# A hybrid attention kernel: where in a tick TensorE adds the logits of the additive attention

## The chip, the cores and the metric

One Trainium2 chip, one of its cores. The metric is the device time of one execution in microseconds (us). Of the kernel before there are three timed runs and one profiled execution. The profiler names the engines PE (TensorE, matrix products), PEld (its weight loads), DVE (VectorE), ACT (ScalarE), POOL (GpSimd) and SP (SyncE, which here only issues DMAs).

## The reference

The input is 16 batches of 768 tokens with 128 channels. Three layers follow one another, each with a residual:

```python
x = x + _L0_conv_ref(_gn(x), ...)        # group norm, 8-head attention with two relative biases and a causal mask
t = t + _L1_attn_ref(_ln_t(t), ...)      # additive attention, below
t = t + _L1_ffn_ref(_ln_t(t), ...)       # 8 experts, top 2, gathered and scattered rows
```

The part that the change touches is the additive attention. With hidden width 16 it computes, for every pair of tokens of a batch:

```python
A = jnp.einsum('bse,he->bsh', q, W1[:, :e]) + b1
B = jnp.einsum('bse,he->bsh', k, W1[:, e:])
hidden = jnp.tanh(A[:, :, None, :] + B[:, None, :, :])
logits = jnp.einsum('bijh,h->bij', hidden, w2) + b2[0]
attn = jax.nn.softmax(logits, axis=-1)
return jnp.einsum('bij,bjd->bid', attn, v)
```

## The kernel before

**Passes, ticks, quarters.** The batches run through a software pipeline of five stages, `pre`, `max`, `mid`, `add` and `end`. A pass handles one stage of each of five consecutive batches; passes 1 to 12 hold all five stages, those before and after hold fewer. A pass is cut into 24 ticks, a tick into four quarters (slot 0 to 3). Every engine walks the ticks in its own program order and meets the others only at semaphores, so "the same tick" may lie several microseconds apart on two engines. After the passes comes the expert part, which the change leaves alone.

**What PE does in a tick.** In each quarter it makes the ring uses that `tick_order` deals out (`fill`): matrix products and transposes into three PSUM banks used in turn. They are called here by their names in the code: `max` (products whose maximum bounds the first attention's scores, L1113), `heads` and `headsT`, `project`, `probsT` (transposes of the second attention's probabilities, L1132), `attended` (their product with the values, L1135), and so on. Behind the uses of quarters 0 and 1 stands half a step of the first attention's scores (`fill_scores`, L1005 and L1008). In quarter 2 stands `weigh_values` (L1021), the product of probabilities and values of the first attention.

**The query groups.** The logits of the additive attention are made for 24 groups q of 32 queries in a pass. POOL adds (`sums`, L833) three quarters of the hidden layer of group q at its tick q, ACT takes the tanh (L954, and L960, which does the last quarter whole) at its tick q, and PE multiplies by w2 (`add_logits`, L1035) at its tick q + 1. `add_logits` has 8 matmuls of 384 columns, each an output strip of 32 columns of the array; `weigh_values` has 4 matmuls in strips of the same kind. All other products use the array's full width. Four groups fill one PSUM region: q % 4 == 0 starts it and waits for ACT's exponential of the four before (`exp_logits`, L938), q % 4 == 3 ends it, after which DVE takes its maximum at slot 1 of the next tick. In the kernel before, groups with q % 4 of 1, 2 and 3 are added at the start of slot 0, those with q % 4 == 0 in slot 2, ahead of `weigh_values`. So with t = q + 1, ticks 1, 5, 9, 13, 17 and 21 have the addition in slot 2, the other eighteen in slot 0.

**The waits around it.** A ring use waits until DVE has read the bank used three uses earlier; `headsT` waits for DVE's reading of `heads`, `attended` for that of `probsT`. Half a score step waits until ACT has taken the exponential (`exp_scores`, L931) of the same half of the step before: ACT does that at the start of its tick, before its tanh. POOL's `sums` of group q wait for the logits of group q - 4, since `hidden` has four slots. At tick 1 SP stores the last block of the `end` batch and then, at tick 2, issues the loads of `q_max`, `k_max`, `q_parts` and `k_parts` (L650); at ticks 0 to 5 and 18 to 23 POOL also issues indirect DMAs of rows (L862), with a drain ahead of the third sum.

Of the kernel before, what the change touches and what calls it, by code (L numbers as in the profile page):

```python
# [47 lines left out]
def score_step(t, first):  # L48

    for stage in ("max", "mid"):  # L50
        d = TICKS * STAGES.index(stage) + t - first
        if 0 <= d < len(STEPS):
            return stage, d
    return None, None
# [58 lines left out]
def tick_order(t):  # L113

    units = list(MAX_AT[t])
    uses = list(AT[t])
    step = max(1, len(units) // max(1, len(uses)))
    out = []
    while units or uses:
        out += units[:step]  # L120
        units = units[step:]
        for _ in range(1 if len(uses) <= 3 else 2):
            if uses:
                out.append(uses.pop(0))
    n = len(out)
    return [out[n * i // PARTS:n * (i + 1) // PARTS] for i in range(PARTS)]
# [37 lines left out]
def positive(count):  # L164

    return not isinstance(count, int) or count > 0


def hybrid_kernel(nc, x, Wq0, Wk0, Wv0, Wo0, rel_t, rel_n, Wq1, Wk1, Wv1, W1, b1, w2, b2,
# [38 lines left out]
    with ctx:  # L208
# [764 lines left out]
        def _(pe):  # L973
# [38 lines left out]
            def weigh_values(c, side, d):  # L1012
                quad, lo, kb, q0, n_ = STEPS[d]
                pe.wait_ge(scores_read, c * 48 + (2 * d + 2))
                group = sum(g < d for g in LAST_OF_GROUP)
                if kb == 0:

                    if positive(count := c * 6 + group):
                        pe.wait_ge(av_copied, count)
                for g in range(4):  # L1020
                    last = mm(av_bank[32 * g:32 * g + 32, q0 - lo:q0 - lo + n_], v_aug[:, side, kb, 4 * quad + g, :],  # L1021
                              probs0[:, d % 3, g, 0:n_], start=(kb == 0), stop=(d in LAST_OF_GROUP),
                              skip_group_check=True)
                last.then_inc(av_done, 1)

            def add_logits(b, q):
                k = q % 4
                pe.wait_ge(tanh_done, b * 24 + (q + 1))
                if k == 0:

                    if positive(count := b * 6 + q // 4):
                        pe.wait_ge(probs1_ready, count)
                for half in range(2):
                    for g in range(4):
                        last = mm(logits[32 * g:32 * g + 32, half, 0:HALF], w2_shifted[:, k, :],  # L1035
                                  hidden[:, q % SLOTS, g, HALF * half:HALF * half + HALF], start=(k == 0), stop=(k == 3))
                last.then_inc(logits_added, 1)

            def keep_warm(n):
                for _ in range(n):  # L1040
                    mm(scores[:, 0, :], ones_bf[0:112, :], bias_q[:, 0, 0:512], start=True, stop=True)
# [117 lines left out]
            def body(ps):  # L1159
                for t in ps.ticks:  # L1160
                    parts = tick_order(t)
                    fill_stage, step = score_step(t, FILL_AT)
                    values_stage, weighed = score_step(t, VALUES_AT)
                    stage, q = ("add", t - 1) if t else ("end", TICKS - 1)
                    for slot in range(PARTS):
                        if slot == 0 and q % 4 and ps.has(stage):
                            add_logits(ps.batch(stage), q)
                        for use in parts[slot]:
                            if ps.has(use[0]):
                                fill(ps, use)  # L1170
                        if slot < 2 and ps.has(fill_stage):
                            fill_scores(ps.batch(fill_stage), step, slot)
                        if slot == 2 and q % 4 == 0 and ps.has(stage):
                            add_logits(ps.batch(stage), q)
                        if slot == 2 and ps.has("add") and not ps.has("mid"):
                            keep_warm(3)
                        if slot == 3 and not ps.has("add") and ps.has("end") and not positive(NB - ps.b):
                            if t in WARM_AT:
                                keep_warm(WARM_AT[t])
                        if slot == 2 and ps.has(values_stage):  # L1180
                            weigh_values(ps.batch(values_stage), ps.side(values_stage), weighed)

            passes(pe, body, prepare)
            expert_products(pe)

# [398 lines left out]
```

## Time and profile before

| | |
|---|---|
| median of 3 runs | 2287.06 us (2283.81 to 2290.32) |
| profiled execution: device time | 2273.98 us |
| profiled execution: span of the core | 2272.2 us |
| mean granted TensorE clock | 0.972 |
| busy: PE, ACT, POOL, DVE | 2061.4, 1676.9, 1565.4, 1550.8 us |
| L1035, additions of logits | 582.8 us busy on PE |
| pass 9 to pass 10, first addition to first addition | 119.5 us, 115.3 us |

The span is the time from the first to the last instruction of the core. A row of the timeline gives start, duration, engine, line, operation and operands; matmuls overlap, so the step from one row's start to the next row's start is what a group costs on PE when there is no idle time between them. A remark in square brackets is idle time just before the row, and what ended it. "issue" there means that the profile shows no event that ended it.

### The profile page before, as it was taken

How to read it: one execution, taken by the hardware profiler on the slowest of the kernel's cores; microseconds unless marked ns; L12 is line 12 of the kernel's file. 1: busy time of each engine (PE TensorE's matmuls, PEld its weight loads, DVE VectorE, ACT ScalarE, POOL GpSimd, SP SyncE). 2: the span in 40 equal slices, each digit the busy share in tenths (PEclk: the TensorE clock that was granted, in tenths of full speed). 3: DMA queues.
4: the chain of work that ended last, by engine and by line, in shares of the span. 5: the costliest groups of instructions: out<-in, count | busy, mean ns of one | idle time of the engine just before them, and what ended most of it. 6: DMA issues, size and time to landing. Idle time of an engine off the chain costs nothing.

```text
span 2272.2 us, 54398 instructions
## 1 busy us (share of the span) xinstructions
PE 2061.4 (91%) x19525; PEld 1206.4 (53%) x19525; DVE 1550.8 (68%) x4147; ACT 1676.9 (74%) x1934; POOL 1565.4 (69%) x1951
## 2 busy tenths in 40 slices
PE   4899999999999999999999999999999977899996
PEld 2555555555555555555555455555554433357775
DVE  7787777777777777777787778787867454324343
ACT  3549888888888888887888788888888978424332
POOL 5127677676767777776767676767677888547777
PEclk8899999999999999999999999999999999899998
DMA  4746413232222222222222322222221000025553
GB/s 120 109 87 149 89 35 78 44 72 47 67 46 65 51 69 47 73 49 72 50 71 51 71 50 64 54 62 52 58 44 26 12 6 5 24 56 87 84 89 34
DMA packets 157428, 137.41 MB, mean 60 GB/s; under 512 B 24665, under 2 KB 149814, under 8 KB 157104
## 3 DMA queue, kind: packets, MB, share of 16 engines
q1 hardware_dynamic: 119376, 109.87, 23.4%
q0 software_dynamic: 23824, 16.85, 5.4%
q10 hardware_dynamic: 13968, 7.30, 1.3%
q8 instruction: 154, 2.52, 0.5%
q14 instruction: 106, 0.87, 0.1%
HBM read 82.68 MB, written 54.52 MB: 60 GB/s over the span
## 4 chain that ended last, share of the span: by engine, by line
PE 26%; POOL 19%; issue 17%; DVE 15%; POOLq 13%; DVEq 5%; ACT 3%; DMA 2%; SPq 0%; ACTq 0%
POOL hidden L833 14%; POOLq L832 10%; PE logits L1035 7%; POOL out_dram L588 4%; DVE max_halves L1307 3%; PE av_bank L1021 3%; PE ring L1113 2%; PE scores L1005 2%; PE scores L1008 2%; PE ring L1135 2%; ACT hidden L954 1%; PE ring L1104 1%; ACT hidden L960 1%; PE ring L1127 1%; DVEq L1389 1%
## 5 line engine op out<-in xcount | busy, mean ns | idle before, releaser
L833 POOL TENSOR_SCALAR hidden<-b_rep,a_cols 128x768 f32<-128x768 f32 x1152 | 1054.7, 919 | 403.1 <-issue 234.8
L954 ACT ACTIVATE hidden<-hidden 128x2304 f32<-128x2304 f32 x384 | 816.9, 2127 | 66.2 <-POOL hidden L833 66.0
L1035 PE MATMUL logits<-hidden,w_shifted 128*32 128x384 f32 x6144 | 582.8, 497 | 61.0 <-ACT hidden L960 29.9
L1307 DVE TENSOR_REDUCE max_halves<-ring 128x4 f32<-128x512 f32 (+1 forms) x704 | 450.7, 659 | 158.9 <-PE ring L1113 158.2
L931 ACT ACTIVATE probs<-scores 128x512 f32<-128x512 f32 (+1 forms) x768 | 391.3, 547 | 196.9 <-PE scores L1008 190.9
L960 ACT ACTIVATE hidden<-b_rep,a_cols 128x768 f32<-128x768 f32 x384 | 358.6, 934 | 0.0
L1035 PEld LDWEIGHTS logits<-hidden,w_shifted 128*32 128x32 f32 x6144 | 163.9, 110 | 294.2 <-issue 233.6
L1113 PE MATMUL ring<-k_max,q_max 112*128 112x128 bf16 x2688 | 270.6, 223 | 13.8 <-DVE max_halves L1307 8.8
L1005 PE MATMUL scores<-bias_q,onehot_k 112*128 112x512 bf16 (+1 forms) x768 | 274.3, 358 | 3.7 <-DMA q_parts<-max_parts 2.1
L1008 PE MATMUL scores<-q_parts,k_parts 98*128 98x256 bf16 (+1 forms) x1536 | 275.6, 260 | 0.0
L1113 PEld LDWEIGHTS ring<-k_max,q_max 112*128 112x128 bf16 x2688 | 181.1, 99 | 154.8 <-issue 58.2
L862 POOL DMA_INDIRECT expert_rows<-rows,slots x198 | 202.4, 1022 | 55.7 <-issue 35.3
L1021 PE MATMUL av_bank<-probs,v_aug 128*32 128x256 f32 (+1 forms) x3072 | 224.7, 363 | 6.1 <-DVE headsT_raw L1479 4.5
L1008 PEld LDWEIGHTS scores<-q_parts,k_parts 98*128 98x128 bf16 x1536 | 152.3, 99 | 87.5 <-issue 15.5
L515 ACT ACTIVATE hidden<-scores,eb1T 128x384 f32<-128x384 f32 x80 | 46.5, 581 | 164.6 <-PE scores L476 161.9
L1135 PE MATMUL ring<-v,probs1T 128*128 128x128 f32 x1152 | 151.1, 282 | 15.1 <-DVE max_halves L1307 12.9
L1135 PEld LDWEIGHTS ring<-v,probs1T 128*128 128x128 f32 x1152 | 138.8, 194 | 28.6 <-DVE max_halves L1307 21.8
L938 ACT ACTIVATE probs<-logits,logit_bias 128x768 f32<-128x768 f32 x96 | 86.8, 904 | 81.9 <-DVE logit_bias L1495 80.0
L1365 DVE COPY probs1T<-ring 128x384 f32<-128x384 f32 x192 | 102.9, 551 | 56.7 <-PE ring L1132 56.3
L1005 PEld LDWEIGHTS scores<-bias_q,onehot_k 112*128 112x128 bf16 x768 | 77.3, 101 | 93.2 <-issue 61.1
L487 PEld LDWEIGHTS logits<-probs,hidden 128*128 128x128 f32 x960 | 113.4, 192 | 12.3 <-issue 2.0
L487 PE MATMUL logits<-probs,hidden 128*128 128x128 f32 x960 | 113.7, 275 | 1.9 <-DVE gn_small L557 1.9
(272 smaller groups left out, 2618.7 us busy)
## 6 DMA issues: line engine op xcount, KB each, us to landing
qk_parts<-qk_parts_sb SPq DMA_DIRECT2D x16, 1152.0 KB, 4.3
q_parts<-qk_parts SPq DMA_DIRECT2D x192, 96.0 KB, 3.2
k_parts<-qk_parts SPq DMA_DIRECT2D x192, 96.0 KB, 4.3
q_max<-qk_parts SPq DMA_DIRECT2D x96, 96.0 KB, 3.0
k_max<-qk_parts SPq DMA_DIRECT2D x96, 96.0 KB, 3.6
expert_rows<-clear_row ACTq DMA_DIRECT2D x9, 792.0 KB, 5.1
x_in<-in_x_dram SPq DMA_DIRECT2D x96, 64.0 KB
x<-in_x_dram SPq DMA_DIRECT2D x96, 64.0 KB
```

Of the source, the lines that this page charges most:

```text
L832: pool.drain()
L833: last = g.tensor_scalar(hidden[:, q % SLOTS, o, :], b_rep[:, side], 1.0, a_cols[:, side, a_col(q, o):a_col(q, o) + 1], ALU.mult, ALU.add)
L931: s.activation(probs0[:, d % 3, 2 * pair:2 * pair + 2, 0:n_], scores[:, pair].rearrange("p (j l) -> p j l", j=2)[:, :, 0:n_], ACT.Exp) \
L954: s.activation(hidden[:, t % SLOTS, 0:3, :], hidden[:, t % SLOTS, 0:3, :], ACT.Tanh)
L960: s.activation(hidden[:, t % SLOTS, 3, :], b_rep[:, side], ACT.Tanh, bias=a_cols[:, side, col:col + 1]).then_inc(tanh_done, 1)
L1005: mm(bank[:, :, 0:n_], onehot_k[:], bias_q[:, h:h + 2, q0 - P * kb:q0 - P * kb + n_], start=True, stop=False, skip_group_check=True)
L1008: last = mm(bank[:, j, 0:n_], k_parts[0:98, h + j, P * kb:P * kb + P], q_parts[0:98, h + j, q0:q0 + n_], start=False, stop=True, skip_grou ...
L1021: last = mm(av_bank[32 * g:32 * g + 32, q0 - lo:q0 - lo + n_], v_aug[:, side, kb, 4 * quad + g, :], probs0[:, d % 3, g, 0:n_], start=(kb = ...
L1035: last = mm(logits[32 * g:32 * g + 32, half, 0:HALF], w2_shifted[:, k, :], hidden[:, q % SLOTS, g, HALF * half:HALF * half + HALF], start= ...
L1113: last = mm(bank[:, P * j:P * j + P], q_max[:, h + j, P * qb:P * qb + P], k_max[:, h + j, P * kb:P * kb + P], start=True, stop=True)
L1135: last = mm(bank[:, 0:P], probs1T[:, P * kb:P * kb + P], v1[:, ps.side(stage), kb, :], start=(kb == 0), stop=(kb == TB - 1))
L1307: v.tensor_reduce(max_halves[:, h % 4:h % 4 + n_, BLOCK_PAIRS.index((qb, kb))], bank[:, 0:n_ * P].rearrange("p (h k) -> p h k", h=n_), AX. ...
```

## The change

Groups with q % 4 of 1 and 2 are added in slot 2 too; only q % 4 == 3 stays in slot 0.

```diff
                     stage, q = ("add", t - 1) if t else ("end", TICKS - 1)
                     for slot in range(PARTS):
-                        if slot == 0 and q % 4 and ps.has(stage):
+                        if slot == 0 and q % 4 not in (0, 1, 2) and ps.has(stage):
                             add_logits(ps.batch(stage), q)
                         for use in parts[slot]:
                             if ps.has(use[0]):
                                 fill(ps, use)
                         if slot < 2 and ps.has(fill_stage):
                             fill_scores(ps.batch(fill_stage), step, slot)
-                        if slot == 2 and q % 4 == 0 and ps.has(stage):
+                        if slot == 2 and q % 4 in (0, 1, 2) and ps.has(stage):
                             add_logits(ps.batch(stage), q)
```

No instruction is added or removed, and only PE's order changes. In a pass twelve additions move, those of ticks 2, 3, 6, 7, 10, 11, 14, 15, 18, 19, 22 and 23.

PE, ticks 14 and 15 of a full pass, before, from `heads` (L1120, end of tick 13) to `attended` (L1135, end of tick 15); L1098 is `headsT`, L1132 `probsT`, L1109 the product `v`, L1125 `project`:

```order
L1120 MATMUL ring<-ident,headsT_raw 128x128 x4
L1035 MATMUL logits<-hidden,w_shifted 32x384 x8
L1113 MATMUL ring<-k_max,q_max 128x128 x4
L1005 MATMUL scores<-bias_q,onehot_k 128x512
L1008 MATMUL scores<-q_parts,k_parts 128x256 x2
L1098 MATMUL ring<-ident,heads 128x128 x3
L1005 MATMUL scores<-bias_q,onehot_k 128x512
L1008 MATMUL scores<-q_parts,k_parts 128x256 x2
L1113 MATMUL ring<-k_max,q_max 128x128 x4
L1021 MATMUL av_bank<-probs,v_aug 32x256 x4
L1132 MATMUL ring<-ident,probs 128x128 x6
L1035 MATMUL logits<-hidden,w_shifted 32x384 x8
```

The same place now:

```order
L1120 MATMUL ring<-ident,headsT_raw 128x128 x4
L1113 MATMUL ring<-k_max,q_max 128x128 x4
L1005 MATMUL scores<-bias_q,onehot_k 128x512
L1008 MATMUL scores<-q_parts,k_parts 128x256 x2
L1098 MATMUL ring<-ident,heads 128x128 x3
L1005 MATMUL scores<-bias_q,onehot_k 128x512
L1008 MATMUL scores<-q_parts,k_parts 128x256 x2
L1113 MATMUL ring<-k_max,q_max 128x128 x4
L1035 MATMUL logits<-hidden,w_shifted 32x384 x8
L1021 MATMUL av_bank<-probs,v_aug 32x256 x4
L1132 MATMUL ring<-ident,probs 128x128 x6
```

The addition of tick 14 moved from behind `heads` to behind the second `max`. That of tick 15 goes the same way, from ahead of that tick's first `max` to behind its second, where it stands ahead of `weigh_values`, `project` and `attended`.

PE, the end of tick 15 before, from the product `v` (L1109) to `attended` (L1135):

```order
L1109 MATMUL ring<-wv,xnT 128x128 x6
L1005 MATMUL scores<-bias_q,onehot_k 128x2x128
L1008 MATMUL scores<-q_parts,k_parts 128x128 x2
L1113 MATMUL ring<-k_max,q_max 128x128 x4
L1021 MATMUL av_bank<-probs,v_aug 32x256 x4
L1125 MATMUL ring<-wo,headsT 128x128 x3
L1135 MATMUL ring<-v,probs1T 128x128 x6
```

And now:

```order
L1109 MATMUL ring<-wv,xnT 128x128 x6
L1005 MATMUL scores<-bias_q,onehot_k 128x2x128
L1008 MATMUL scores<-q_parts,k_parts 128x128 x2
L1113 MATMUL ring<-k_max,q_max 128x128 x4
L1035 MATMUL logits<-hidden,w_shifted 32x384 x8
L1021 MATMUL av_bank<-probs,v_aug 32x256 x4
L1125 MATMUL ring<-wo,headsT 128x128 x3
L1135 MATMUL ring<-v,probs1T 128x128 x6
```

The addition now stands between the tick's last `max` and the products L1021, L1125 and L1135.

PE, tick 18 before, from its addition to `weigh_values`:

```order
L1035 MATMUL logits<-hidden,w_shifted 32x384 x8
L1005 MATMUL scores<-bias_q,onehot_k 128x512
L1008 MATMUL scores<-q_parts,k_parts 128x256 x2
L1113 MATMUL ring<-k_max,q_max 128x128 x4
L1005 MATMUL scores<-bias_q,onehot_k 128x512
L1008 MATMUL scores<-q_parts,k_parts 128x256 x2
L1132 MATMUL ring<-ident,probs 128x128 x3
L1021 MATMUL av_bank<-probs,v_aug 32x256 x4
```

And now:

```order
L1005 MATMUL scores<-bias_q,onehot_k 128x512
L1008 MATMUL scores<-q_parts,k_parts 128x256 x2
L1113 MATMUL ring<-k_max,q_max 128x128 x4
L1005 MATMUL scores<-bias_q,onehot_k 128x512
L1008 MATMUL scores<-q_parts,k_parts 128x256 x2
L1132 MATMUL ring<-ident,probs 128x128 x3
L1035 MATMUL logits<-hidden,w_shifted 32x384 x8
L1021 MATMUL av_bank<-probs,v_aug 32x256 x4
```

The tick now begins with the first half of the scores, and tick 19, whose order is alike, does too.

## Rows read from the trace of the kernel before

**Rows 1.** Busy times by stretch (us; instruction counts; granted PE clock, DMA share, GB/s).

```profile
350.00:1700.00 1350.00, 1272.42 (x13048) 716.48 (x13044) 1040.77 (x2670) 1128.12 (x1271) 971.89 (x1268) 1.00 0.28 59
1018.00:1025.00 7.00, 5.38 (x43) 3.47 (x41) 5.65 (x16) 3.39 (x4) 3.17 (x4) 0.76 0.00 0
```

**Rows 2.** Waits of PE, 350 to 1700 us: who for whom, us in total, times, longest.

```profile
PE logits L1035 <- ACT hidden L960: 20.1, 34, 1.2
```

**Rows 3.** Timeline of PE, pass 10, ticks 9 and 10.

```profile
1239.67 0.39 PE L1113 MATMUL ring<-k_max,q_max 112*128 112x128 bf16 x4
1239.99 1.50 PE L1035 MATMUL logits<-hidden,w_shifted 128*32 128x384 f32 x16
1241.30 0.61 PE L1021 MATMUL av_bank<-probs,v_aug 128*32 128x256 f32 x8
1241.85 0.91 PE L1104 MATMUL ring<-xnT,wq 128*128 128x384 f32 x2
...
1243.02 1.50 PE L1035 MATMUL logits<-hidden,w_shifted 128*32 128x384 f32 x16
1244.45 0.40 PE L1113 MATMUL ring<-k_max,q_max 112*128 112x128 bf16 x4
```

**Rows 4.** Timeline of DVE, pass 10, ticks 9 and 10.

```profile
1243.91 0.55 DVE L1337 COPY headsT<-ring 128x384 f32<-128x384 f32 x1
1244.88 0.69 DVE L1307 TENSOR_REDUCE max_halves<-ring 128x4 f32<-128x512 f32 x1 [0.42 <-PE ring L1113]
```

**Rows 5.** Timeline of PE, pass 10, ticks 14 and 15.

```profile
1263.77 0.40 PE L1113 MATMUL ring<-k_max,q_max 112*128 112x128 bf16 x4
1264.00 0.38 PE L1005 MATMUL scores<-bias_q,onehot_k 112*128 112x512 bf16 x1
...
1265.01 0.55 PE L1098 MATMUL ring<-ident,heads 128*128 128x128 f32 x3 [0.41 <-DVE heads L1332]
...
1266.15 0.64 PE L1021 MATMUL av_bank<-probs,v_aug 128*32 128x256 f32 x8
1266.72 0.87 PE L1132 MATMUL ring<-ident,probs 128*128 128x128 f32 x6
1267.52 1.50 PE L1035 MATMUL logits<-hidden,w_shifted 128*32 128x384 f32 x16
...
1271.62 0.64 PE L1021 MATMUL av_bank<-probs,v_aug 128*32 128x256 f32 x8
1272.19 0.94 PE L1125 MATMUL ring<-wo,headsT 128*128 128x128 f32 x6
```

**Rows 6.** Timeline of DVE, pass 10, ticks 14 and 15.

```profile
1268.75 1.01 DVE L1365 COPY probs1T<-ring 128x384 f32<-128x384 f32 x2
...
1273.17 0.56 DVE L1342 TENSOR_TENSOR x<-ring,x 128x384 f32<-128x384 f32 x1 [0.40 <-PE ring L1125]
```

**Rows 7.** Timeline of PE, pass 10, ticks 18 and 19.

```profile
1282.59 1.50 PE L1035 MATMUL logits<-hidden,w_shifted 128*32 128x384 f32 x16 [0.70 <-ACT hidden L960]
1284.02 0.39 PE L1005 MATMUL scores<-bias_q,onehot_k 112*128 112x512 bf16 x1
...
1289.87 1.60 PE L1135 MATMUL ring<-v,probs1T 128*128 128x128 f32 x12
```

**Rows 8.** Timeline of ACT, pass 10, start of tick 18.

```profile
1282.44 1.07 ACT L931 ACTIVATE probs<-scores 128x512 f32<-128x512 f32 x2
```

**Rows 9.** Timeline of SP, pass 10, tick 2.

```profile
1198.48 1.45 SPq L650 DMA_DIRECT2D q_max<-qk_parts  x3
```

**Rows 10.** Timeline of POOL, pass 10, tick 4.

```profile
1213.78 0.91 POOL L833 TENSOR_SCALAR hidden<-b_rep,a_cols 128x768 f32<-128x768 f32 x1 [4.20 <-issue]
```

**Rows 11.** Timeline of ACT, pass 10, tick 7.

```profile
1230.51 2.13 ACT L954 ACTIVATE hidden<-hidden 128x2304 f32<-128x2304 f32 x1 [2.95 <-POOL hidden L833]
```

**Rows 12.** Timeline of PE, pass 10, tick 8.

```profile
1233.51 1.50 PE L1035 MATMUL logits<-hidden,w_shifted 128*32 128x384 f32 x16 [0.93 <-ACT hidden L960]
```
**Rows 13.** Timeline of PE, pass 7, tick 11.

```profile
1020.57 2.89 PE L1135 MATMUL ring<-v,probs1T 128*128 128x128 f32 x12 [0.84 <-DVE max_halves L1307]
```

## The prediction

> **What bounds the kernel now.** I read three views in this order: the busy times by stretch, the waits, and the timelines of one full pass (pass 10, ticks 0 to 23 from about 1196.9 to 1316 us).
>
> The busy times say that PE is the fullest engine: in the stretch of the full passes it is busy 1272 of 1350 us, ACT 1128, DVE 1041, at a granted clock of 1.00 [rows 1]. That suggests that whatever PE is spared is gained. The waits contradict it: PE's largest is for ACT's tanh, 20.1 us in 34 waits [rows 2]. Each wait is a place where PE stands at the end of someone else's chain, and time that PE saves before such a place only lengthens the wait. So I walk one pass and ask which engine sets each stretch:
>
> - Tick 22 of one pass to tick 8 of the next. SP issues its bulk loads at 1198.48 once the last block has been read at the end of tick 23 [rows 9]. POOL stands still for 4.20 us until 1213.78, which I lay to these loads since a POOL DMA lies before its drain, and then runs through to the sums of group 7 [rows 10]. ACT waits 2.95 us for those sums [rows 11], PE 0.93 us for ACT [rows 12]. This stretch is PE's up to the store, then SP's, the DMAs' and POOL's.
> - Ticks 8 to 10 are PE's: DVE waits for it, last at 1244.88, 0.42 us [rows 4].
> - From there to the middle of tick 15 DVE works without a gap, and PE waits for it, as at `headsT`, 0.41 us [rows 5].
> - In tick 15 PE takes over: DVE waits 0.40 us for `project` [rows 6]. By way of `attended`, the maximum of the logits and ACT's exponential the chain comes to the tanh that the addition of tick 18 waits 0.70 us for [rows 7]. PE leads on from there to `attended` of tick 19, and DVE to tick 21.
>
> **The change part by part.** *What an addition costs in either place.* Followed by full-width work it takes 1244.45 - 1243.02 = 1.43 us, followed by `weigh_values` 1241.30 - 1239.99 = 1.31 us [rows 3]: 0.12 us less. Entering a strip group costs too: `max` takes 1239.99 - 1239.67 = 0.32 us ahead of an addition [rows 3] and 1264.00 - 1263.77 = 0.23 us ahead of scores [rows 5], so 0.09 us, paid once instead of twice. `weigh_values` behind an addition takes 1241.85 - 1241.30 = 0.55 us by the start of the next group, against 1266.72 - 1266.15 = 0.57 us on its own [rows 3, 5], 0.02 us. Leaving takes some 0.01 us once less. Together 0.24 us for each moved addition, 12 x 0.24 = 2.9 us a pass of PE's own work.
>
> The Trainium skill, page "TensorEngine Tiling (Array Packing)", section "Key Properties", says that a change of tiling mode, not merely of tile, drains TensorE. By that rule, the trace agrees: the full-to-strip change costs 0.09 us and the way back 0.12 us. The rule speaks for the change, and would by itself make it worth the whole 2.9 us a pass; rival 1 is what then follows.
>
> *What the move does to the order.* The work of slots 0 to 2 now comes one addition earlier, 1.43 + 0.09 = 1.5 us, and everything in slot 3 stands where it stood, unless PE waited in between. Where it did, the addition no longer hides in that wait but comes behind it. That is the price, and I work it out per stretch and pass.
>
> *A, ticks 22 to 8.* Ticks 22 and 23 lie ahead of SP's store, so two moved additions bring the loads, and with them POOL's chain, forward by 2 x 0.24 = 0.5 us. The savings of ticks 2, 3, 6 and 7 end in the wait at tick 8. Since `attended` of tick 7 must await a copy of DVE and now has the addition behind it, PE may come late itself. Bounds -0.5 and 0; I take -0.4 us, nearer the first, since PE has 0.93 us to spare there in this pass [rows 12].
>
> *B, tick 10.* Its first `max` no longer waits behind the addition. DVE ends its copy of `headsT` at 1243.91 + 0.55 = 1244.46 and had to wait until 1244.88 [rows 4]; now it goes on at once. -0.42 us, and not more, because the copy before comes from tick 9, where nothing moves. Bounds -0.42 and 0.
>
> *C, ticks 14 and 15.* `headsT` starts at 1265.01 when DVE lets it, whether an addition stands ahead or not; PE's wait there grows from 0.41 us to 0.41 + 1.5 = 1.9 us. The addition of tick 14 now comes behind it and delays `probsT` from 1266.72 by 1.31 - 0.02 = 1.29 us to 1268.0, finished 0.87 us later at about 1268.9 [rows 5]. DVE first touches those two banks at 1268.75 [rows 6], and needs only the first of them then: just hidden. In place of the addition at 1267.52 come the `max` and `v`, which await DVE as before, so this tick's second `max`, just ahead of L1021, stands where it stood. Behind it, though, is the second moved addition: L1021 and `project`, which started at 1271.62 and 1272.19, start 1.29 us later, and DVE was already waiting for `project` [rows 6]. +1.29 us. The bound below is 0, if DVE's queue were longer than it looks; above, 2 x 1.29 = 2.6 if the delay of `probsT` showed as well. I take 1.29.
>
> *D, ticks 16 to 19.* All is 1.29 us late up to the tanh. PE no longer waits for that tanh (0.70 us) [rows 7]. But now the first half of the scores stands foremost, and it needs ACT's exponential of the same half of the step before, the first of the two that start at 1282.44 and last 1.07 us together: ready at about 1282.44 + 0.54 = 1282.98, an estimate from half of that row [rows 8]. The addition used to cover just this. So scores start, with 0.06 us for the signal, 0.45 us behind the old addition's start of 1282.59 instead of 1284.02 - 1282.59 = 1.43 us behind it. From the scores to `attended` PE took 1289.87 - 1284.02 = 5.85 us, 1.48 of it (with its entry) the addition of tick 19 [rows 7]. Now it takes 5.85 - 1.48 + 2 x 1.29 = 6.95 us, and `attended` comes 0.45 + 6.95 = 7.40 us behind the mark where it came 7.28. +0.12 us: the two savings and the lost wait are used up by two additions in the way of `attended` and by the uncovered exponential. Bounds: -1.2 (0.70 of the wait and 2 x 0.24 kept) and +0.5.
>
> POOL's and DVE's other dependences hide: the sums of group q need the logits of group q - 4, and POOL is early by more than an addition in every tick outside A, where the additions needed are also earlier. The tail (batch 15 alone) is paced by POOL and ACT; nothing there for or against.
>
> *Sum.* -0.4 - 0.42 + 1.29 + 0.12 = +0.59 us a pass. Passes 1 to 12 are full, and pass 0 and pass 13 are nearly so; I count 13. 13 x 0.59 = +7.7 us on 2273.98 us, 2282 us. The profiled execution is 13.1 us (0.6%) below the median of the timed runs, so I add the difference to the median: 2287.06 + 7.7 = 2295.
>
> **The rivals.**
>
> *1. PE's work sets the time (faster).* For it: 94% busy, and DVE and ACT wait for PE at many places too [rows 1, 4]. Then all additions with `weigh_values` behind them save: 14 passes of 12 and 6 in pass 14, 174 x 0.24 = 42 us, 2245 us. If the vanished waits for tanh are gained too (0.7 us at tick 18 in pass 10, at most 20.1 us in all [rows 2, 7]), 2225. A part of it, stretch D at its lower bound and C hidden by half, gives -0.4 - 0.42 + 0.65 - 1.2 = -1.4 us a pass, 18 us, 2269. Against it: rows 5, 6, 11 and 12, where PE is not what the next step waits for.
>
> *2. It cancels (no change).* If C costs only about 0.7 us, the sum is 0: 2287. For it: the margins at `probsT` and in A are tenths of a microsecond.
>
> *3. Slower through TensorE's clock.* In one pass, at tick 11, PE stood idle for DVE for 0.84 us ahead of a group [rows 13], and the stretch around it shows a granted clock of 0.76, so part of it at 1.2 instead of 2.4 GHz [rows 1]. The new wait of 1.9 us in tick 14 is longer than that one. If the clock fell in every third pass and 5 us of work took 3 us longer, that is 4 x 3 = 12 us more: 2307. Against it: tick 11's wait gets shorter, for the same reason as C's gets longer.
>
> **How the numbers follow.** A measurement of this kernel tells 0.3%, 6.9 us, from no change. The forecast case has a chance of 0.45 (2287 to 2305; slower by over 0.3% in 0.29, within it in 0.16). Rival 1 has 0.26, all but 0.01 faster. Rival 2 has 0.14, of it 0.11 within 0.3% and 0.03 slower. Rival 3 has 0.15, slower. Faster 0.25, same 0.28, slower 0.47. The bounds of the terms add to -0.5 - 0.42 + 0 - 1.2 = -2.1 and 0 + 0 + 2.6 + 0.5 = +3.1 us a pass, -28 and +40 us: 2259 to 2327. Rival 3 and the forecast end well below that top, so the range is 2255 to 2315, which leaves out most of rival 1's full form. The forecast's own range is 2287 to 2305.
>
> **What the profile after would show.** A: the wait at tick 8 shrinks to nearly nothing. B: DVE's maximum in tick 10 follows the copy of `headsT` without a gap. C: a wait of about 1.9 us ahead of `headsT` in tick 14, and DVE's wait ahead of `project` in tick 15 of 1 us or more. D: a wait of PE ahead of L1005 in tick 18 for ACT's L931, and none ahead of the addition. In sum: PE's busy time falls by some 40 us while its waits grow by more. Wrong would be: passes of the middle shorter by 1 us or more (then PE's work counts), `project` of tick 15 no later, or granted clock below 1.00 in several passes.

## The result, and the profile after

| | before | after |
|---|---|---|
| median, us | 2287.33 (2283.81 to 2290.32, 4 runs) | 2322.27 (2317.71 to 2327.38, 4 runs) |
| profiled execution, its span, us | 2273.98, 2272.2 | 2325.46, 2323.7 |
| PE busy in the span, us | 2061.4 | 2052.2 |

The ratio is 1.0159, 95% interval 1.0133 to 1.0184: 35 us slower. The forecast was 2295, the range ended at 2315.

The first part of the page after (busy time, share of the span, instructions), and the stretch of the full passes as in [rows 1]:

```profile
PE 2052.2 (88%) x19525; PEld 1236.1 (53%) x19525; DVE 1553.7 (67%) x4147; ACT 1671.2 (72%) x1934; POOL 1560.4 (67%) x1951
350.00:1700.00 1350.00, 1227.60 (x12656) 718.65 (x12655) 1013.92 (x2606) 1089.41 (x1234) 938.77 (x1227) 0.99 0.28 57
```

PE is busy 9 us less in a longer span: it saved some work, and more waiting came in. PE's waits in that stretch (who for whom, us in total, times, longest), to be read against [rows 2]:

```profile
PE scores L1005 <- ACT probs L931: 35.1, 41, 1.2
PE ring L1098 <- DVE heads L1332: 21.6, 11, 2.3
PE ring L1127 <- DVE headsT L1337: 11.4, 12, 1.3
```

The wait for the tanh, 20.1 us before, is gone from the list. In its place stand scores that wait for ACT's exponential, and `headsT` that waits for DVE's `heads`, once a pass, 2.0 us in the mean (before 4.8 us in 11 waits). The third line is what it was before, 11.4 us.

I put both traces' PE instructions beside the program order and took the start of each tick from the start of its pass, as a mean over the twelve full passes. A pass takes 115.92 us before and 119.27 after, +3.35:

| stretch | ticks 0 to 7 | 8, 9 | 10, 11 | 12, 13 | 14, 15 | 16 to 19 | 20, 21 | 22, 23 |
|---|---|---|---|---|---|---|---|---|
| after - before, us | +0.86 | -0.08 | -0.13 | +0.05 | +2.41 | +0.45 | +0.06 | -0.27 |

Two thirds and more lie in ticks 14 and 15. This is PE there, in the pass that rows 3 to 12 are from. The rows and the prediction call it pass 10; it is the ninth of the twelve full ones, the longest before (119.5 us), with one of that trace's two falls of the clock, at its tick 20. Before, its ticks 14 and 15 take 1262.34 to 1274.40 = 12.06 us, here 1293.25 to 1307.56 = 14.31:

```profile
1293.25 0.39 PE L1113 MATMUL ring<-k_max,q_max 112*128 112x128 bf16 x4
...
1296.00 0.55 PE L1098 MATMUL ring<-ident,heads 128*128 128x128 f32 x3 [1.93 <-DVE heads L1332]
...
1297.14 1.50 PE L1035 MATMUL logits<-hidden,w_shifted 128*32 128x384 f32 x16
1298.46 0.61 PE L1021 MATMUL av_bank<-probs,v_aug 128*32 128x256 f32 x8
1299.00 0.87 PE L1132 MATMUL ring<-ident,probs 128*128 128x128 f32 x6
...
1300.87 1.58 PE L1109 MATMUL ring<-wv,xnT 128*128 128x128 f32 x12 [0.55 <-DVE probs1T L1365]
...
1303.17 0.40 PE L1113 MATMUL ring<-k_max,q_max 112*128 112x128 bf16 x4 [0.49 <-DVE max_halves L1307]
1303.50 1.50 PE L1035 MATMUL logits<-hidden,w_shifted 128*32 128x384 f32 x16
1304.81 0.61 PE L1021 MATMUL av_bank<-probs,v_aug 128*32 128x256 f32 x8
1305.36 0.94 PE L1125 MATMUL ring<-wo,headsT 128*128 128x128 f32 x6
```

Measured from `headsT`: `probsT` starts 3.00 us behind it where it was 1.71 [rows 5], +1.29 as predicted. `project` starts 9.36 us behind it where it was 7.18, +2.18 instead of the predicted 1.29. The two new waits ahead of `v` and of the second `max`, both for DVE, hold the 0.89 us between. (From `headsT` to `project` PE stands idle for 1.04 us in this pass, where it stood idle for 0.05 before.) DVE and POOL in the same stretch, after:

```profile
1297.77 0.56 DVE L1391 CAST qk_parts_sb<-xT 128x768 bf16<-128x768 f32 x1
1298.25 0.69 DVE L1307 TENSOR_REDUCE max_halves<-ring 128x4 f32<-128x512 f32 x1
1299.02 1.24 DVE L1394 TENSOR_TENSOR qk_parts_sb<-xT,qk_parts_sb 128x384 bf16<-128x384 f32 x1
1300.18 1.01 DVE L1365 COPY probs1T<-ring 128x384 f32<-128x384 f32 x2
1301.28 1.23 DVE L1394 TENSOR_TENSOR qk_parts_sb<-xT,qk_parts_sb 128x384 bf16<-128x384 f32 x1
```

```profile
1298.95 0.91 POOL L833 TENSOR_SCALAR hidden<-b_rep,a_cols 128x768 f32<-128x768 f32 x1 [2.96 <-PE logits L1035]
1300.02 1.01 POOL L833 TENSOR_SCALAR hidden<-b_rep,a_cols 128x768 f32<-128x768 f32 x1 [0.17 <-issue]
1301.20 0.91 POOL L833 TENSOR_SCALAR hidden<-b_rep,a_cols 128x768 f32<-128x768 f32 x1 [0.17 <-issue]
```

And before, the rows of both engines that stand there:

```profile
1266.78 0.81 DVE L1391 CAST qk_parts_sb<-xT 128x768 bf16<-128x768 f32 x1
...
1268.27 0.56 DVE L1394 TENSOR_TENSOR qk_parts_sb<-xT,qk_parts_sb 128x384 bf16<-128x384 f32 x1
...
1269.86 0.78 DVE L1394 TENSOR_TENSOR qk_parts_sb<-xT,qk_parts_sb 128x384 bf16<-128x384 f32 x1
```

```profile
1267.34 1.01 POOL L833 TENSOR_SCALAR hidden<-b_rep,a_cols 128x768 f32<-128x768 f32 x1 [0.17 <-issue]
1269.33 0.91 POOL L833 TENSOR_SCALAR hidden<-b_rep,a_cols 128x768 f32<-128x768 f32 x1 [0.97 <-PE logits L1035]
```

L1394 is DVE's `split`, which makes the bf16 parts of q and k. Alone it takes 0.56 us; begun 0.07 us behind one of POOL's sums of 0.91 us it takes 1.24. POOL's sums of group 17 need the logits of group 13, and these are the addition of tick 14, which now stands behind the 1.93 us wait. So POOL waits 2.96 us and starts just as DVE comes to its splits. The two splits are longer by 0.68 and 0.45 us, L1391 is shorter by 0.25: +0.88, the missing 0.89 us. The Trainium skill, page "SBUF — State Buffer", section "SBUF: two separate sides", says that VectorE and GpSimd share a pair of ports as an exclusive lock: an instruction of VectorE with two SBUF inputs and one of GpSimd that reads SBUF don't share it, the later one waits until the other is done. The trace agrees. Wherever a split begins inside one of POOL's sums, up to 0.67 us after its start, it ends 0.40 us after that sum, no matter when it began. In the rows above the second split before ends at 1269.86 + 0.78 = 1270.64, POOL's sum at 1270.24; the two after end at 1300.26 and 1302.51, POOL's sums at 1299.86 and 1302.11. So the split is not slowed down. It waits, and the profile shows the waiting as a longer instruction and not as idle time.

That is one kind of pass. In six of the twelve, TensorE's clock fell behind the wait instead. The granted clock of such a tick 14 (columns as in [rows 1]) and its PE and DVE rows:

```profile
1178.00:1183.00 5.00, 4.61 (x34) 2.06 (x34) 3.70 (x9) 4.15 (x5) 0.41 (x2) 0.66 0.00 0
```

```profile
1178.39 0.57 PE L1098 MATMUL ring<-ident,heads 128*128 128x128 f32 x3 [1.93 <-DVE heads L1332]
...
1180.17 2.47 PE L1035 MATMUL logits<-hidden,w_shifted 128*32 128x384 f32 x16
```

```profile
1181.41 0.56 DVE L1394 TENSOR_TENSOR qk_parts_sb<-xT,qk_parts_sb 128x384 bf16<-128x384 f32 x1
1183.59 1.02 DVE L1365 COPY probs1T<-ring 128x384 f32<-128x384 f32 x2 [1.62 <-PE ring L1132]
1184.71 0.64 DVE L1394 TENSOR_TENSOR qk_parts_sb<-xT,qk_parts_sb 128x384 bf16<-128x384 f32 x1
```

Part of this stretch runs at 1.2 GHz: the addition takes 2.47 instead of 1.50 us, POOL's sums come later still, miss the splits (0.56 and 0.64 us), and DVE waits 1.62 us for `probsT` instead. The two costs take each other's place: without the fall ticks 14 and 15 last 14.31 to 14.34 us in five passes and 14.66 in one (one that is longer before, too: 12.96 instead of 12.06), with it 14.64 to 14.76 us in five and 15.36 in one.

### The profile page after: what moved, and what is told of

Same layout as the page of the kernel before. It is cut to its first block, busy times and chain, and to the rows that moved or that the text cites. A ratio compares the mean times of both kernels' runs of the same rounds, so it can differ in the third digit from the quotient of the medians.

```text
span 2323.7 us, 54398 instructions
## 1 busy us (share of the span) xinstructions
PE 2052.2 (88%) x19525; PEld 1236.1 (53%) x19525; DVE 1553.7 (67%) x4147; ACT 1671.2 (72%) x1934; POOL 1560.4 (67%) x1951
## 4 chain that ended last, share of the span: by engine, by line
PE 23%; POOL 20%; issue 19%; DVE 14%; POOLq 14%; DVEq 5%; ACT 3%; DMA 2%; another core or an unknown queue 0%; SPq 0%; ACTq 0%
POOL hidden L833 15%; POOLq L832 11%; PE logits L1035 7%; POOL out_dram L588 4%; DVE max_halves L1307 3%; PE av_bank L1021 2%; PE ring L1113 2%; PE scores L1005 2%; PE scores L1008 2%; PE ring L1104 1%; PE ring L1135 1%; PE ring L1127 1%; ACT hidden L954 1%; PE ring L1139 1%; PE logits L487 1%
## 5 line engine op out<-in xcount | busy, mean ns | idle before, releaser
L1035 PE MATMUL logits<-hidden,w_shifted 128*32 128x384 f32 x6144 | 588.8, 502 | 31.9 <-ACT probs L938 27.8
L1113 PEld LDWEIGHTS ring<-k_max,q_max 112*128 112x128 bf16 x2688 | 191.2, 99 | 95.8 <-DVE max_halves L1307 37.9
L1021 PE MATMUL av_bank<-probs,v_aug 128*32 128x256 f32 (+1 forms) x3072 | 220.5, 358 | 8.1 <-DVE headsT_raw L1479 7.0
L1135 PE MATMUL ring<-v,probs1T 128*128 128x128 f32 x1152 | 151.4, 282 | 10.8 <-DVE probs1T L1365 10.0
L1021 PEld LDWEIGHTS av_bank<-probs,v_aug 128*32 128x32 f32 x3072 | 89.1, 110 | 127.8 <-issue 114.0
L1135 PEld LDWEIGHTS ring<-v,probs1T 128*128 128x128 f32 x1152 | 138.6, 194 | 25.5 <-DVE probs1T L1365 13.3
```

Of the source, the lines that this page charges most:

```text
L1113: last = mm(bank[:, P * j:P * j + P], q_max[:, h + j, P * qb:P * qb + P], k_max[:, h + j, P * kb:P * kb + P], start=True, stop=True)
L1135: last = mm(bank[:, 0:P], probs1T[:, P * kb:P * kb + P], v1[:, ps.side(stage), kb, :], start=(kb == 0), stop=(kb == TB - 1))
```

## The experiments

The theory after the two traces: the loss is made by the additions of ticks 14 and 15, one by `project`'s delay (the predicted mechanism), the other by POOL's sums moved beside DVE's splits, or by the clock. Rivals: each moved addition costs alike; the clock alone. Unless said otherwise a kernel is the one before with another set of ticks whose addition stands in slot 2; the condition for slot 0 is its opposite. "Ticks 14+15" is the length of these two in the profiled run, over the full passes.

**All but 14 and 15.**

```
-                        if slot == 0 and q % 4 and ps.has(stage):
+                        if slot == 0 and t not in (1, 2, 3, 5, 6, 7, 9, 10, 11, 13, 17, 18, 19, 21, 22, 23) and ps.has(stage):
-                        if slot == 2 and q % 4 == 0 and ps.has(stage):
+                        if slot == 2 and t in (1, 2, 3, 5, 6, 7, 9, 10, 11, 13, 17, 18, 19, 21, 22, 23) and ps.has(stage):
```

> The changed kernel with the additions of ticks 14 and 15 back in slot 0. Theory (the loss is made in ticks 14 and 15, where the addition comes behind TensorE's wait for headsT and delays probsT, v and project): the passes lose their 2.2 to 2.4 us each in these ticks no longer, 13 x 2.3 = 30 us of the 35 come back, 2292 (2286 to 2299). Rival (every moved addition costs a little, the places are interchangeable): 2 of 12 come back, some 6 us, 2316. Rival (additions put late elsewhere hold POOL's sums back and cost there): 2300 to 2310.

2290.71 us, ratio to before 1.0009 (0.9986 to 1.0031). The loss is gone with these two.

**Only 14 and 15.**

```
+                        if slot == 2 and t in (1, 5, 9, 13, 14, 15, 17, 21) and ps.has(stage):
```

> The kernel before with the additions of ticks 14 and 15 alone moved to slot 2. Theory: the loss of these ticks and the clock's falls there, 13 x 2.3 = +30 us, 2317 (2308 to 2322). Rival (every moved addition costs a little): 2/12 of 35 = +6 us, 2293.

2327.31 us, 1.0172 (1.0126 to 1.0218). They make all of it; ticks 14+15 take 14.60 us in the mean, as after the change. The median lies above the expected span, which ended at 2322.

**The wait filled.** The changed kernel, and:

```
                 elif name == "headsT":
+                    if i == 1:
+                        if positive(count := ps.number(use) - (RING - 1)):
+                            pe.wait_ge(ring_read, count)
+                        for _ in range(8):
+                            mm(bank[:, 0:HALF], ones_bf[0:112, :], bias_q[:, 0, 0:HALF], start=True, stop=True)
                     after("heads", 1 + i)
```

> The changed kernel, and ahead of the second headsT of tick 14 eight matmuls of 384 columns whose result is overwritten, 1.3 us of work in the wait of 1.96 us. Rival 3 of the prediction (the clock falls through this wait and makes the pass longer): the falls at tick 14 go, and 5 to 12 us come back, 2310 to 2317. Theory (the passes in which the clock fell were only 0.4 us longer, and half of them had it): 2 to 3 us at most, within 0.3% of the changed kernel, 2319 to 2323.

2314.74 us, 1.0116 (1.0067 to 1.0165), an interval that touches the changed kernel's: by time alone undecided between the two. The trace says more. No clock falls in tick 14 any more, and every pass now has the stretched splits (mean 1216 ns over 24; before the change it is 672 over 24, after it 950 over 22):

```profile
L1399 DVE TENSOR_TENSOR qk_parts_sb<-xT,qk_parts_sb 128x384 bf16<-128x384 f32 x24 | 29.2, 1216 | 2.6 <-issue 0.4
```

Ticks 14+15 take 14.32 us in eleven passes of twelve, 14.35 in the mean against 14.60. So with the falls a pass costs 0.25 us more in the mean than with what takes their place.

**22 to 7.**

```
+                        if slot == 2 and t in (1, 2, 3, 5, 6, 7, 9, 13, 17, 21, 22, 23) and ps.has(stage):
```

> The kernel before with the additions of ticks 22, 23, 2, 3, 6 and 7 alone moved. The prediction's term A: -0.4 us a pass, 13 passes, 2282. What the two traces suggest (ticks 22 and 23 shorter by 0.27 us, ticks 0 to 7 longer by 0.86): +0.6 us a pass, 2295. Within 0.3% of 2287 would mean neither.

2295.78 us, 1.0038 (1.0012 to 1.0064): a small loss where term A of the prediction had a small gain.

**Only 14; only 15.**

```
+                        if slot == 2 and t in (1, 5, 9, 13, 14, 17, 21) and ps.has(stage):
```

> The kernel before with the addition of tick 14 alone in slot 2. The prediction's term C gave this half nothing: the delay of probsT just hidden, 2287. New theory: this addition releases POOL's sums of group 17, which now run beside DVE's split in tick 14 (0.56 and 0.79 us become 1.23 and 1.23 us) and make probsT, v and the maximum 1 us late: 13 x 1.0 = +13 us, and a few more for the clock in later ticks, 2301 (2297 to 2308). Rival (the 39 us of both additions are the delay of project by the second): 2287 to 2290.

2305.88 us, 1.0087 (1.0066 to 1.0108).

```
+                        if slot == 2 and t in (1, 5, 9, 13, 15, 17, 21) and ps.has(stage):
```

> The kernel before with the addition of tick 15 alone in slot 2. The prediction's term C: L1021 and project come 1.29 us later and DVE waits for project already, 13 x 1.29 = +17 us. New theory: the same, and the rest of the 39 us lies with tick 14 or after, 2304 (2300 to 2312). Rival (the two losses are one and need both moves): 2290 to 2297.

2308.81 us, 1.0085 (1.0052 to 1.0118). Both medians lie in the expected spans, but the traces give a different reason for the first.

With 14 alone, ticks 14+15 take 13.15 to 13.18 us in eight passes, and the splits are stretched as in the pair. Yet from `headsT` to `project` it is 1282.66 - 1274.47 = 8.19 us, +1.01, and PE does not wait for DVE once on the way:

```profile
1274.47 0.55 PE L1098 MATMUL ring<-ident,heads 128*128 128x128 f32 x3 [1.93 <-DVE heads L1332]
...
1277.49 1.23 DVE L1394 TENSOR_TENSOR qk_parts_sb<-xT,qk_parts_sb 128x384 bf16<-128x384 f32 x1
...
1282.66 0.94 PE L1125 MATMUL ring<-wo,headsT 128*128 128x128 f32 x6
```

So here the stretch is hidden, and the price is the addition itself, which PE now makes behind the wait. In the other four passes the clock fell and they take 14.71 to 15.13.

With 15 alone, ticks 14+15 take 13.10 to 13.14 us in ten passes, and no split is stretched (mean 558 ns). From `headsT` to `project` it is 1291.91 - 1283.67 = 8.24 us, +1.06, and PE stands idle for 1.22 us of it, waiting for DVE where the addition used to be.

```profile
1283.67 0.55 PE L1098 MATMUL ring<-ident,heads 128*128 128x128 f32 x3 [0.40 <-DVE heads L1332]
...
1290.05 1.50 PE L1035 MATMUL logits<-hidden,w_shifted 128*32 128x384 f32 x16
1291.91 0.94 PE L1125 MATMUL ring<-wo,headsT 128*128 128x128 f32 x6
```

The two ratios add up to the pair's 1.0172, but that is no sign that the pair's loss is made of these two parts. The next runs show that it is not.

**POOL's sums out of the way, and the control.** Ticks 14 and 15 moved, and (alone, for the control):

```
-                    last = g.tensor_scalar(hidden[:, q % SLOTS, o, :], b_rep[:, side], 1.0,
+                    n_ = 8 if q == 17 else L
+                    last = g.tensor_scalar(hidden[:, q % SLOTS, o, 0:n_], b_rep[:, side, 0:n_], 1.0,
```

> Ticks 14 and 15 moved, as in the run with these two alone (2327), and POOL's three sums of group 17 are made for 8 of the 768 columns only (the rest of that group's hidden values is left as it was), so that nothing of POOL stands beside DVE's split in tick 14. To be read against the same edit on the kernel before. Theory (DVE's split, stretched beside POOL, is 1 us of the 3 us lost a pass): about 13 us below 2327, 2313, and 26 us above its control. Rival (the stretch is hidden, TensorE's own lateness counts): no change, 2325 to 2329, and 39 us above its control.

> The control: the kernel before with POOL's sums of group 17 made for 8 of 768 columns only. In it DVE's split is stretched from 0.56 to 0.8 us in one or two of three instructions a pass, beside sums of groups 17 and 18: at most 0.5 us a pass come back. 2281 to 2288 by either theory.

2310.44 us, 1.0094 (1.0071 to 1.0117), and for the control 2286.89 us, 0.9985 (0.9961 to 1.0008). The pair of moves now costs 23.6 us instead of 39. The splits of tick 14 in the first:

```profile
L1395 DVE TENSOR_TENSOR qk_parts_sb<-xT,qk_parts_sb 128x384 bf16<-128x384 f32 x23 | 13.1, 570 | 2.5 <-issue 0.4
```

Without a fall of the clock ticks 14+15 take 13.06 or 13.07 us in six passes of seven, in the control 12.05: +1.01. So the stretch is 14.31 - 13.06 = 1.25 us of the 2.25. (That is more than the 0.88 above, because the stretches that the kernel before has there are gone too.) PE then never waits for DVE between `headsT` and `project`: the delay by the addition of tick 14 gives DVE the time that PE has to wait for with tick 15 alone. So without the stretch the two moves together cost what either costs alone, and the stretch makes the rest. Where the clock falls it is 14.7, another +1.6, with no stretched split for it to replace.

**Tick 14's addition inside the wait.**

```
+                        if slot == 1 and t == 14 and ps.has(stage):
+                            add_logits(ps.batch(stage), q)
```

> The kernel before with the addition of tick 14 alone moved, and only to slot 1, ahead of the second headsT, so that it still lies in the time in which TensorE waits for DVE there. Theory (the loss comes from standing behind this wait): nearly nothing, since probsT is not late; POOL's sums of group 17 start some 1.3 us later and may stretch one of DVE's splits, 0 to 0.5 us a pass, 2287 to 2295. Rival (any delay of this addition costs what slot 2 costs): 2301 to 2306, as with tick 14 in slot 2.

2283.92 us, 1.0012 (0.9990 to 1.0034): ahead of the wait the addition costs nothing that can be measured, behind it 0.87%. From `headsT` to `project` it is 7.18 us again, and the splits (mean 674 ns) are as before. What counts is the side of `headsT` on which it stands.

**Neither stretch nor fall.** Ticks 14 and 15 moved, with the short sums and the filling.

```
+                    n_ = 8 if q == 17 else L
...
+                        for _ in range(8):
+                            mm(bank[:, 0:HALF], ones_bf[0:112, :], bias_q[:, 0, 0:HALF], start=True, stop=True)
```

> Ticks 14 and 15 moved, POOL's sums of group 17 made for 8 of 768 columns, and eight matmuls of 384 columns in TensorE's wait ahead of headsT. With neither a stretched split nor a fall of the clock in tick 14, only the delay of project by the second addition should be left, which the prediction priced at 1.29 us: 13 x 1.2 to 1.3 = 16 us over the control with short sums (2287), 2303 (2299 to 2307), and no pass whose ticks 14 and 15 are longer than 13.5 us. Rival (a third cost is in it): 2310 as without the filling, or more.

2303.77 us, which was the number expected, but by luck: the kernel before ran at 2281.90 in this group of runs, so the ratio is 1.0118 (1.0089 to 1.0147; the two medians make 1.0096) where 1.007 was meant. Half right: ticks 14+15 take 13.06 or 13.07 us in ten passes, 13.42 at most, 1.01 over the control, so nothing else is in them. But the clock then fell at ticks 20 and 21 in five of twelve passes (control: three), and the time won in tick 14 does not show in the timed runs.

**22 and 23; 2 to 7.**

```
+                        if slot == 2 and t in (1, 5, 9, 13, 17, 21, 22, 23) and ps.has(stage):
```

> The kernel before with the additions of ticks 22 and 23 alone moved. The prediction's term A gave these two 0.5 us a pass, carried to tick 8: 2281. The traces (ticks 22 and 23 shorter by 0.27 us): 2283 to 2285. Rival (POOL's sums, held back by later additions, eat it): 2287 or more.

2275.98 us, 0.9980 (0.9962 to 0.9997): a gain of 0.2%, near the traces' 0.27 us a pass (0.15% over 13 passes).

```
+                        if slot == 2 and t in (1, 2, 3, 5, 6, 7, 9, 13, 17, 21) and ps.has(stage):
```

> The kernel before with the additions of ticks 2, 3, 6 and 7 alone moved. The prediction's term A had them at nothing (their savings end in the wait of tick 8). The runs of 22 to 7 (+0.38%) and of 22 and 23 (-0.20%) leave +0.58% for them, 2300 (2294 to 2306): the scores of ticks 2, 6 and 7 now wait for ACT's exponentials without cover, and attended of tick 7 stands behind the addition. Rival (the prediction's): 2284 to 2290.

2293.31 us, 1.0014 (0.9998 to 1.0029). My 2300 was a miss: the price is at most half of what I subtracted from two other runs. Such differences of differences are finer than the runs are.

**10, 11, 18, 19, 22 and 23.**

```
+                        if slot == 2 and t in (1, 5, 9, 10, 11, 13, 17, 18, 19, 21, 22, 23) and ps.has(stage):
```

> A version that may beat the kernel before: the additions of ticks 10, 11, 18, 19, 22 and 23 alone moved. If the moves add up: all but 14 and 15 gave 2291, those of 22 to 7 gave 2296, so 10, 11, 18 and 19 are worth 5 us, and 22 and 23 some 3 us: 2279 (2275 to 2284). Rival (the two runs differ by chance and these four are worth nothing): 2284 to 2288.

2269.27 us, 0.9951 (0.9934 to 0.9969): faster than both kernels, and below the expected span (2275 to 2284), partly because all runs of this group are some 5 us faster. These six moves put no addition between a wait for DVE and what DVE waits for next. But its profiled passes, 115.88 us, are no shorter than the 115.92 of before. Where the gain lies, its profile doesn't show.

**The kernel before, profiled again, and the waits of ticks 20 and 21 filled.** No edit for the first. For the second, and for the third with the six moves:

```
                 elif name == "x1T":
+                    if i == 0:
+                        if positive(count := ps.number(use) - (RING - 1)):
+                            pe.wait_ge(ring_read, count)
+                        for _ in range(2):
+                            mm(bank[:, 0:HALF], ones_bf[0:112, :], bias_q[:, 0, 0:HALF], start=True, stop=True)
...
                 elif name in ("A", "B", "V"):
+                    if name == "B" and i == 0:
+                        if positive(count := ps.number(use) - (RING - 1)):
+                            pe.wait_ge(ring_read, count)
+                        for _ in range(4):
+                            mm(bank[:, 0:HALF], ones_bf[0:112, :], bias_q[:, 0, 0:HALF], start=True, stop=True)
```

> The kernel before, unchanged, profiled once more. If the number of falls of TensorE's clock in the full passes varies between executions, this profile has more than two of them and a span nearer to the timed 2287 (2280 or more). If not, two falls again and a span of 2272 within 0.2%.

> The kernel before with two matmuls of 384 columns ahead of x1T in tick 20 and four ahead of B in tick 21, both in waits of TensorE (0.64 and 0.95 us in the mean), their results overwritten. Theory (timed runs lose some 13 us to falls of the clock there, of which the profiled one had few): 2272 to 2280. Rival (the falls come at another place instead, or cost nothing on the path): 2284 to 2290.

> The same filling on the version with ticks 10, 11, 18, 19, 22 and 23 moved, which came out 0.49% below the kernel before. If this version's gain is that it has fewer falls already (one in its profile): 2266 to 2272, nothing more. If the two add: 2258 to 2266.

The kernel before, profiled again, has a span of 2293.6 us, 21.4 more than the profile that the prediction rests on. Five falls of the clock stand in its full passes instead of two, a pass takes 116.62 us instead of 115.92, and ticks 0 to 7 alone 0.41 us more, with nothing changed. Half of term A's +0.86 is thus within what two executions of one kernel differ by. Filling ticks 20 and 21 gave 2287.78 us, 0.9989 (0.9977 to 1.0001), the rival's number: one fall stands there (one and three in the two profiles without the filling), but tick 20 itself took 0.9 us longer (6.66 against 5.78), since the filling does not always meet a wait. With the six moves it gave 2275.40 us, 0.9940 (0.9923 to 0.9956), which cannot be told from 0.9951 without it. That the clock takes 13 us of the timed runs in those two ticks, the theory of this run, is not shown.

## Why the prediction was wrong

The direction was right, and so was the reason for it: PE is the fullest engine and still does not set the time. The step that failed is in term C, "POOL's and DVE's other dependences hide". In its place the runs show DVE's splits waiting beside POOL's sums, 1.25 us of the 2.25 that ticks 14 and 15 are longer in a pass without a fall.

By the profiles the sum is +3.35 us a pass instead of +0.59. Of the missing 2.76 us C has 1.1, A 1.0, B and D 0.3 each. By the timed runs C weighs more: the pair of moves costs 39 us where C had 17, and the other ten moves together 3 us (-3 to +7) where A, B and D had -9.

- **Cost of an addition in either place.** As predicted (1297.14 to 1298.46 is 1.32 us), and PE's busy time fell, though by 9 us and not 40. In the passes without a fall of the clock it is 107.26 us (three after) against 108.84 (ten before), 1.58 less and not 2.9; why not more is open. The nine passes after with a fall have 108.95, since groups at the lower clock last longer. What the prediction took from the Trainium skill, page "TensorEngine Tiling (Array Packing)", section "Key Properties", that a change of tiling mode drains TensorE, was true of PE's work and without effect on the time, except in ticks 22 and 23: these two are 0.27 us shorter, where 2 x 0.24 = 0.48 was forecast.
- **B.** DVE's maximum follows the copy without a gap, as said:

```profile
1274.85 0.55 DVE L1337 COPY headsT<-ring 128x384 f32<-128x384 f32 x1
1275.32 0.69 DVE L1307 TENSOR_REDUCE max_halves<-ring 128x4 f32<-128x512 f32 x1
```

  Yet ticks 10 and 11 give 0.13 us, not 0.42. The 0.42 us are won and lost again to the mechanism of C: DVE's six short instructions on two SBUF operands there (L1412 to L1435, 0.21 us each when alone) take 3.59 us a pass instead of 3.11 in the mean, because they now meet POOL's sums more often. Where one of them is stretched, it ends 0.05 us behind the sum that it met:

```profile
1276.00 0.91 POOL L833 TENSOR_SCALAR hidden<-b_rep,a_cols 128x768 f32<-128x768 f32 x1 [0.17 <-issue]
...
1276.45 0.51 DVE L1412 TENSOR_TENSOR rt<-rt,rs 128x48 f32<-128x48 f32 x1
...
1279.18 0.96 POOL L833 TENSOR_SCALAR hidden<-b_rep,a_cols 128x768 f32<-128x768 f32 x1 [1.20 <-PE logits L1035]
...
1279.44 0.75 DVE L1433 SCALAR_TENSOR_TENSOR rt<-rt 128x48 f32<-128x48 f32 x1
```

- **C**, the step that failed. Forecast +1.29, measured +2.41 in the profile, 31 us over 13 passes. Much of its PE side was right: wait 1.93 against 1.9, `probsT` 1.29 later, "just hidden" (DVE reads it at 1300.18, when its own split ends, and not when PE is done), DVE's wait ahead of `project` well over 1 us:

```profile
DVE x L1342 <- PE ring L1125: 20.3, 12, 1.7
```

  What failed is the sentence "POOL's and DVE's other dependences hide". I asked whether POOL would be late for ACT. I did not ask beside what it would now run. Before, POOL's three sums of group 17 run from 1265.18 to 1268.35, and DVE's first split begins at 1268.27. From `headsT` on they begin 0.17 us behind it before and 2.95 after; moved by 2.8 us they lie on both splits. Without this, the pair costs 1.01 us. That it is near 1.29 is partly luck: "which await DVE as before" does not hold, since PE stood idle for only 0.05 us in all between `headsT` and `project` before, and with the short sums for 0.00 in six of seven passes without a fall. So moving the addition of tick 14 alone, which C had at nothing, costs 1.01 us too.
- **D.** The exchange happened (the scores of tick 18 wait for ACT, 1.08 us in the mean, and the addition no longer does), and costs 0.45 us instead of 0.12. About 0.3 of it is the split at tick 16, two instructions a pass, stretched beside POOL's sums (1054 ns in the mean against 916), and comes from tick 15: with that addition alone moved, ticks 16 to 19 are 0.29 us longer. With 18 and 19 moved and 14 and 15 not, they are 0.14 us longer, so D's own number was nearly right. The pass that it was read from was not typical, though: the wait for the tanh is 0.70 us there and 0.44 or 0.45 in the other eleven.
- **A.** Forecast -0.4, profile +0.59, timed +0.14% for ticks 2 to 7 and -0.20% for 22 and 23. The wait at tick 8 shrank as predicted, from 0.56 to 0.07 us in the mean (0.93 in the pass that was read). The exponentials uncovered in ticks 2 and 6 (0.34 and 1.19 us ahead of the scores, where 0.08 and 0.70 stood ahead of the additions) are the mechanism of term D, which I had worked out for tick 18 and not looked for here. `attended` of tick 7 waits for DVE, 0.62 us in the mean and not at all before, which the prediction had named as a possibility.
- **Rival 3, the clock,** was half true: it does fall behind the 1.9 us wait, in half of the passes. It costs little on top (0.25 us a pass), because it moves POOL's sums off the splits; where the splits are not stretched, or their stretch is hidden as with tick 14 alone, it is 1.6 us each time. It was a rival and belonged beside the forecast as a second case of the same tick.
- **The range.** The bounds of my own terms reached to 2327, and 2322 lies inside. I ended at 2315 because I thought that the ends would not come together. C alone came out at 2.41 of its 2.6.

Not settled: where the 0.5% of the version with six moves comes from, and what the falls at ticks 20 and 21 cost in timed runs.

## What to carry to other kernels

Work moved behind a wait is late by the whole wait for everyone who needs it, so follow each of its consumers to the instructions that they will then run beside, not only to those that they will wait for. Where instructions of two engines hold each other up, the distance between them in the trace is a margin like any other: here nothing was left of it after a move of 2.8 us. Such waiting shows in no list of waits, only in the duration of the same instruction in two traces (672 ns in the mean against 950). Where PE has slack ahead of a wait, put extra work ahead of it (no measurable cost here) and not behind (0.9%).

## What was unexpected of the hardware

- DVE's subtraction of two SBUF operands, 128 x 384 to bf16, took 0.56 us alone and 1.23 us when it started 0.08 us behind a POOL instruction of 0.91 us. Begun inside such an instruction, it ended 0.40 us behind it, whether it began 0.08 or 0.67 us after it; 128 x 48 ended 0.05 us behind it.
- TensorE's granted clock fell in six of twelve passes behind an idle time of 1.93 us, did not in the other six behind 1.93 to 2.28 us, and fell there in none when 1.47 us of it were filled. With that place filled, it fell at later, shorter waits in more passes than before: the number of falls in the full passes was 2 and 5 in two profiles of one kernel.
